# An expert's fourth item gets a body of its own, the loop over further items starts at the fifth

## The reference

```python
order = jnp.argsort(-probs, axis=-1)
sp = jnp.take_along_axis(probs, order, axis=-1)
cum = jnp.cumsum(sp, axis=-1)
exceed = cum > top_p
first_idx = jnp.argmax(exceed, axis=-1)
first = jnp.arange(probs.shape[-1])[None, :] == first_idx[:, None]
kept = jnp.where(~exceed | first, sp, 0.0)
...
for e in range(n_exp):
    g = jax.nn.silu(x @ gate_w[e].T)
    u = x @ up_w[e].T
    y = g * u @ down_w[e].T
    out = out + y * w[:, e:e + 1]
```

## Time and profile before

| what | value |
|---|---|
| median of three runs | 504.88 us (502.75 to 507.34) |
| time of the profiled execution | 506.65 us |
| its span, first to last instruction | 504.8 us |
| mean granted TensorE clock | 0.969 |

### The profile page before, as it was taken

How to read it: one execution, slowest core, us unless ns; L and a number is a source line. 1 busy time by engine, 2 the same in 40 slices (tenths; PEclk the granted TensorE clock), 3 DMA queues, 4 the chain that set the end, 5 groups by cost and what they waited for, 6 DMA issues and landing times. The chain is left out here.

```text
span 504.8 us, 10001 instructions
## 1 busy us (share of the span) xinstructions
PE 464.7 (92%) x3468; PEld 352.6 (70%) x3468; DVE 337.8 (67%) x787; ACT 259.2 (51%) x358; POOL 197.3 (39%) x234
## 2 busy tenths in 40 slices
PE   7787989999999999999999999899989999999982
PEld 7354334345444544445898999899989999999982
DVE  5497496579757977768899758745753857455450
ACT  2235778875877678776552245524332435343330
POOL 4242023003000300003234566565675576766645
PEclk8897999999989999999999999989999999999997
DMA  8601304801001100222336347774754655544533
GB/s 262 207 1 32 95 1 41 126 3 43 2 0 45 42 2 1 86 84 85 109 108 186 69 103 177 212 176 90 194 85 97 162 112 115 110 82 108 82 68 44
DMA packets 30785, 46.01 MB, mean 91 GB/s; under 512 B 3588, under 2 KB 22276, under 8 KB 30728
## 3 DMA queue, kind: packets, MB, share of 16 engines
q0 software_dynamic: 11936, 22.50, 25.0%
q1 hardware_dynamic: 18792, 22.77, 13.7%
HBM read 34.44 MB, written 12.93 MB: 94 GB/s over the span
## 5 line engine op out<-in xcount | busy, mean ns | idle before, releaser
L619 ACT ACTIVATE probs<-psS 128x1024 f32<-128x1024 f32 x128 | 123.2, 1027 | 21.9 <-PE psS L1440 21.5
L1677 PE MATMUL psS<-hs_hi,w_hi 128*128 128x256 f32 x400 | 114.9, 287 | 6.5 <-DVE hs_lo L1220 3.9
L1677 PE MATMUL psS<-hs_hi,w_lo 128*128 128x256 f32 x400 | 113.9, 285 | 0.0
L1677 PE MATMUL psS<-hs_lo,w_hi 128*128 128x256 f32 x400 | 113.8, 284 | 0.0
L480 POOL DMA_INDIRECT out<-y_sel,idx_out x44 | 78.3, 1780 | 39.7 <-DVE y_sel L1257 28.2
L1677 PEld LDWEIGHTS psS<-hs_hi,w_hi 128*128 128x128 f32 x400 | 76.9, 192 | 8.5 <-issue 7.8
L1677 PEld LDWEIGHTS psS<-hs_lo,w_hi 128*128 128x128 f32 x400 | 76.8, 192 | 0.0
L1677 PEld LDWEIGHTS psS<-hs_hi,w_lo 128*128 128x128 f32 x400 | 76.8, 192 | 0.0
L466 POOL DMA_INDIRECT h_sel<-h_rows,idx_in x50 | 53.9, 1078 | 44.1 <-DVE sel L1226 20.2
L1543 PE MATMUL psY<-probs,v_aug 128*32 128x512 f32 x512 | 70.0, 619 | 0.0
L671 ACT ACTIVATE silu_g<-psS 128x512 f32<-128x512 f32 x50 | 29.6, 597 | 67.8 <-PE psS L1677 67.4
(11 more groups left out here) (203 smaller groups left out, 734.4 us busy)
## 6 DMA issues: line engine op xcount, KB each, us to landing
w_in<-gateT SPq DMA_DIRECT2D x8, 512.0 KB, 5.0
w_in<-upT SPq DMA_DIRECT2D x8, 512.0 KB, 4.1
w_in<-downT SPq DMA_DIRECT2D x8, 512.0 KB, 4.5
h_rows<-h_nat SPq DMA_DIRECT2D x4, 528.0 KB, 3.1
x_all<-x SPq DMA_DIRECT2D x4, 512.0 KB, 5.8
h_rows<-mod_table POOLq DMA_DIRECT2D x4, 512.0 KB, 14.9
out<-x_all SPq DMA_DIRECT2D x4, 512.0 KB, 2.9
mod_rows<-mod_table SPq DMA_DIRECT2D x3, 512.0 KB, 5.3
```

Of the source, the lines that this page charges most:

```text
L619: act.activation(probs[:, gk % 4, 2 * pair:2 * pair + 2, :], psS[:, pair, :, :], ACT.Exp, scale=ATT_SCALE).then_inc(probs_done, 1)
L1677: mm = pe.matmul(ps[:, i * SW:(i + 1) * SW], w, v[:, k, :], start=at == 0, stop=at == 3 * KC - 1)
```

## The change

In the walk, for experts 2 to 7, the fourth item gets a body in line under the condition n > 3, and the loop over further items starts at i = 4 and stands under a condition of its own, n > 4. All four engines that walk items run this code. In POOL's write_list the place in the list is addressed from a slice that starts S * (EARLY - 2) = 4 elements into idx_all, with a register value smaller by as much; for items with a fixed number the slice is a constant.

```diff
@@ -289,7 +289,9 @@
                         with eng.If(n > 2):
                             body(e, False, before + 2)
                             with eng.If(n > 3):
-                                others(3)
+                                body(e, False, before + 3)
+                                with eng.If(n > 4):
+                                    others(4)
 
 
         @block.sync
@@ -466,10 +468,14 @@
                     pool.indirect_dma_start(h_sel[:, k, :], None, h_rows[0:rows, :],
                                             bass.IndirectOffsetOnAxis(ap=idx_in[:, k:k + 1], axis=0)).then_inc(gathered, 16)
 
+            early_on = idx_all[:, S * (EARLY - 2):]
+
             def write_list(m):
 
                 pool.wait_ge(scattered, GATES + 32 * m)
-                pool.tensor_copy(idx_out[:, :], idx_all[:, bass.ds(S * m, S)]).then_inc(out_listed, 1)
+
+                place = idx_all[:, S * m:S * (m + 1)] if isinstance(m, int) else early_on[:, bass.ds(S * (m - EARLY + 2), S)]
+                pool.tensor_copy(idx_out[:, :], place).then_inc(out_listed, 1)
```

## The result

The changed kernel takes 513.17 us (median of 4 runs, 511.02 to 517.69). Its ratio to the kernel before is 1.0158, with a 95% interval of 1.0098 to 1.0217: 8 us slower. The forecast was 502.3 us, in a range up to 507.0; the result has the other sign and lies above the range. A fourth execution of the kernel before took 1477.04 us and is in neither its median nor the ratio. What happened is close to the rival that the prediction gave 0.13, two leaps that land in code which is not there, with a third one and a higher price each.

The account below looks back on a forecast made before the run. TensorE's own instruction stream was taken to bound the kernel. Removing the 2.54 us hole after expert 3's fourth item, all other terms 0, took the median 504.88 us to 502.3 us; range 500.9 to 507.0.

Parts of the forecast that it names:

- the rival that the prediction gave 0.13: Ends of experts 4 and 5: two leaps wait for code, costing 3.4 us against 2.54 gained; 505.7 us, chance 0.13.
- What bounds the kernel: In the walk only TensorE's own instruction stream sets the time; any hole opened or closed there moves the end equally.
- The fourth item's body: Expert 3's fourth item on TensorE: same 76 matmuls, and the loop entry saved is hidden; nothing gained or lost.
- the end of the fourth item: After expert 3's fourth item, one n > 4 branch replaces 3.2 us of tests; the 2.54 us hole goes.
- what is late next: After expert 3, hs_lo is ready 1.5 us early and gathered rows 1.3 us early, so the gain is booked whole.
- write_list: POOL's list copy: at most one 0.05 us register operation more or fewer per item; 0, bounds -0.1 and +0.1 us.
- The same body in line for experts 2 and 4 to 7: The n > 3 leap grows from 167 to 326 instructions; branch cost taken as unchanged, 0 us added.
- a rival with 0.28 and 0.13: Leaps land in code not there: expert 4's alone costs 1.7 us, 504.0 us, chance 0.28; two miss, chance 0.13.

Follow-up runs that it names:

- only the body for expert 3: Changed kernel with the fourth body in line for expert 3 alone, the other experts keeping the loop from the third index on: 502.36 us, ratio 0.9946 to the kernel before.
- the two runs with the place set: Changed kernel with a directive setting where the walk's TensorE code starts in a 256-instruction block: at 168, 506.67 us, ratio 1.0001; at 0, 515.66 us, ratio 1.0159.
- the other: The changed kernel measured and profiled once more, without any edit: 511.86 us over 10 runs, ratio 1.0121 to the kernel before.
- a loop with the right end: Kernel before with the loop over further items ending at n instead of 8 and no condition inside: 502.06 us, ratio 0.9914.
- place 0: Changed kernel with TensorE's walk code set to start at the first instruction of a 256-instruction block: 515.66 us, ratio 1.0159 to the kernel before.

## Why the prediction was wrong

**What bounds the kernel** held. TensorE's own stream sets the time, and each hole that opened or closed in it moved the end by its length.

**The fourth item's body, the end of the fourth item, what is late next, write_list** held: the hole of 2.54 us went whole, the gathers were in time, the list copy did nothing that can be measured. With the leaps out of the way the forecast change of -2.5 us is what only the body for expert 3 measures, -2.7 us (0.9946).

**The same body in line for experts 2 and 4 to 7** is the step that failed: a leap of twice the length was priced as the short one. It read: "The cost of the branch itself I take as unchanged, 0.2 to 0.35 us, inside the 0.4 us in hand." Three of the five branches took 3.8, 2.8 and 1.4 us, holes of 5.9 us in sum, and the clock took 4.6 us more in the profiled execution. The evidence for this stood in the prediction, as a rival with 0.28 and 0.13, down to the experts 4 and 5 as the place. I preferred the other reading because of one observation: no code packet while the loop's branches went back and forth. The loop of expert 3 does span a boundary: by the compiled program's count one lies 3 to 26 places behind its first instruction, if it lies where the short and long branches of all runs let it. Its branches from 375.1 to 378.1 took 86 to 232 ns, and no packet of q8 comes from 369.4 to 385.5, so in this stretch a block already passed was still there. I took it as a sign that blocks ahead are there too, and it says nothing about them.

**The rival's price** was too low as well, by three terms. First, I let the branch go on at the end of the packet, 2.1 us late. It goes on 1.4 us later than that: a full miss is 3.8 to 4.2 us in the branch and 3.1 to 3.5 us of hole, not 1.7. Second, I counted a leap into the next block as safe unless the present one had just been entered. As I read the runs, the next block is asked for on entry and needs the same 3.8 us: in the two runs with the place set, a packet of q8 starts 0.7 to 1.8 us after the end of each of the 15 branches that land in another block, takes 0.9 to 1.5 us, and the 11 waits above end some 1.4 us behind a packet; an estimate from 152 matmul and weight-load instructions in 9 us is that the sequencer goes some 65 instructions in 3.8 us. By the count in the compiled program expert 5's leap starts 18 to 41 places behind a boundary and expert 6's 56 to 79, and both waited: the branches took 2.8 and 1.4 us. Expert 6 I had not named. Third, the clock: 1.7 us for one hole, which is the 7.45 us of the group behind the hole at 326 less the usual 5.75, at a granted clock of 0.69 from 328.9 to 332.4, was meant as a possibility; it took 2.8 and 1.8 us in the profiled execution and 2.7 and 0 in the other.

**The chances** were thus wrong by more than the step: the case of two misses was priced at 505.7 us, 507.4 with the clock. With the measured holes of experts 4 and 5 and the clock behind both it would have been 504.88 - 2.54 + 3.1 + 2.1 + 4.6 = 512.1; expert 6's 0.6 makes it 512.7, and 513.17 was measured. That the slower side was among the rivals at all is not luck, since the place and the cause were named; that it was given 0.13 is the miss.

## What to carry to other kernels

Code that is not executed can cost time by lying between a branch and its target: where a sequencer is barely ahead of its engine (0.4 us here), count the instructions that a taken branch leaps over. On TensorE a leap of some 160 took 0.2 to 0.4 us at every place tried, and one of some 320 took 0.3 to 4.2 us depending on where it lay. Before writing out another round of a loop, look at what the loop's rounds do: here four empty tests were the whole cost, and a loop with the right end (0.9914, 0.9879 to 0.9948) gave at least as much as the body in line without the loop behind it (0.9922, 0.9898 to 0.9945), with less code.

## What the runs showed of the hardware

- TensorE's code comes in packets of 16.4 KB, 33 of them in the kernel before. Its compiled program has 8,423 instructions for TensorE, which is 32.9 times 256. Of the prediction's sum of 8,450, the 350 control instructions are 354 records in the trace.
- The packets come one by one with the blocks. At place 0, from 295 us to the end, TensorE enters 19 blocks by the count and q8 brings 22 packets: one for each block, and one more for each of the three leaps past the next one.
- Each of the five leaps past the next block without a hint brought a packet of its own, and went on 3.8 to 4.2 us after it began. The packet itself takes 0.9 to 1.4 us of that and the time behind it 1.4 to 1.5.
- In the walk of the kernel before TensorE's sequencer was at most 21 matmuls ahead of the engine: at the branch at 347.50, 20 matmuls were handed over and not done, and the first one behind it starts at 349.59, 2.1 us later.
- A leap that stayed in its block took 219 to 262 ns, one into the next block 322 to 434 ns where nothing waited much. One position of the boundaries in the code, and in two runs the position that the directive sets, fits all of them.
- Straight code seems to wait for its next block too. At place 0, expert 5's leap took 322 ns but landed near the end of a block. Four matmuls into the next group TensorE had a hole in the middle of its own instructions (chain of waits):

```profile
440.94 0.47 PE psS L1683 x4
441.41 1.07 issue
442.48 3.62 PE psS L1683 x28
```

- That this hole is the wait for the block after the one leapt into is my reading. A packet of q8 lies in 439.6 to 441.4, and the matmuls go on 1.1 us after its end; no experiment separated it.
- A hint 159 instructions ahead of the branch removed a wait of 3.8 us where the leap passed a whole block (expert 4), and did not help where the target was the next block (expert 5, 2.25 us). Each is one leap in one execution.
